# Seven block products for k and v of the second mixer, a halved first piece of expert weights, and two places of the order

## The reference

```python
def heads(t):
    return t.reshape(b, n, h, d).transpose(0, 2, 1, 3)
q = _phi(heads(x @ Wq + bq))          # _phi(t) = elu(t) + 1
k = _phi(heads(x @ Wk + bk))
v = heads(x @ Wv + bv)
kv = jnp.einsum('bhnd,bhne->bhde', k, v)
...
```

```python
importance = jax.lax.stop_gradient(probs).sum(axis=0)
...
balanced = topk_probs / balance
balanced = balanced / balanced.sum(axis=-1, keepdims=True)
```

## Time and profile before

| | us |
|---|---|
| median of 3 runs | 2670.67 |
| lowest, highest | 2668.65, 2671.88 |
| the profiled execution, its own time | 2667.01 |
| its span in the profile | 2665.3 |
| TensorE busy | 2586.9 |
| VectorE busy | 1546.5 |
| ScalarE busy | 780.0 |
| mean granted clock of TensorE | 0.993 of 2.4 GHz |

### The profile page before, as it was taken

How to read it: one execution, slowest core, us unless ns; L and a number is a source line. 1 busy time by engine, 2 the same in 40 slices (tenths; PEclk the granted TensorE clock), 3 DMA queues, 4 the chain that set the end, 5 groups by cost and what they waited for, 6 DMA issues and landing times.

```text
span 2665.3 us, 26854 instructions
## 1 busy us (share of the span) xinstructions
PE 2586.9 (97%) x10727; PEld 1835.0 (69%) x10727; DVE 1546.5 (58%) x2637; ACT 780.0 (29%) x1314; POOL 347.5 (13%) x197
## 2 busy tenths in 40 slices
PE   7999999999999998999999999999999999999999
PEld 4667676658966987777777775555755786556676
DVE  4556461799947996988888997121342561341322
ACT  1043342017723763322222222420002331432000
POOL 0888888000000000000000000000000000000000
PEclk9999999999999998999999999999999999999999
DMA  8232313542020305000120004000350100212201
GB/s 253 29 40 13 49 5 46 146 145 75 20 59 12 104 19 194 1 1 1 71 101 1 24 24 172 11 0 36 79 161 18 36 1 1 69 69 84 86 24 58
DMA packets 137285, 155.70 MB, mean 58 GB/s; under 512 B 96508, under 2 KB 107606, under 8 KB 135634
## 3 DMA queue, kind: packets, MB, share of 16 engines
q1 hardware_dynamic: 66441, 153.56, 18.5%
q0 software_dynamic: 70720, 0.43, 2.7%
...
## 4 chain that ended last, share of the span: by engine, by line
PE 51%; DVE 7%; ACT 2%; DMA 1%; issue 1%; SPq 0%; DVEq 0%; ACTq 0%
PE psum L517 51%; DVE arena L1834 2%; DVE arena L1836 1%; DVE arena L1835 1%; DVE arena L1827 0%; ACT arena L1100 0%; ACT arena L1105 0%; ACT arena L991 0%; DVE arena L1492 0%; DVE arena L1900 0%; PE psum L528 0%; DVE arena L1334 0%; DVE arena L1833 0%; DVE arena L1826 0%; DVE arena L1859 0%
## 5 line engine op out<-in xcount | busy, mean ns | idle before, releaser
L517 PE MATMUL psum<-arena 128*125 128x384 f32 (+10 forms) x9816 | 2478.1, 414 | 39.3 <-DMA arena<-in_ffn_w 7.9
L517 PEld LDWEIGHTS psum<-arena 128*125 128x125 f32 (+3 forms) x9816 | 1733.3, 188 | 758.3 <-issue 135.7
L2161 POOL DMA_INDIRECT count_matrix<-arena x170 | 342.8, 2017 | 118.9 <-DVE arena L1431 59.4
L1834 DVE RECIPROCAL arena<-arena 128x500 f32<-128x500 f32 x60 | 196.7, 3278 | 2.1
L1584 DVE CUSTOM_DVE_ANT_0 arena<-arena 125x1250 bf16<-125x1250 bf16 (+1 forms) x100 | 139.2, 1457 | 12.9 <-ACT arena L1133 12.3
L2171 POOL MEMSET arena<- 125x60 f32 x1 | 0.2, 207 | 980.5 <-PE psum L517 980.5
L1668 DVE TENSOR_TENSOR arena<-arena 125x1250 f32<-125x1250 f32 x80 | 116.3, 1453 | 18.6 <-ACT arena L1082 18.3
L1079 ACT ACTIVATE arena<-arena 125x1250 f32<-125x1250 f32 x80 | 106.9, 1336 | 53.5 <-PE psum L517 53.2
L1671 DVE SCALAR_TENSOR_TENSOR arena<-arena 125x1250 f32<-125x1250 f32 x80 | 116.9, 1461 | 2.8
L991 ACT ACTIVATE arena<-psum 128x250 f32<-128x250 f32 (+1 forms) x102 | 40.8, 491 | 239.6 <-PE psum L528 239.2
L1225 ACT ACTIVATE arena<-psum,arena 128x250 f32<-128x250 f32 x120 | 49.2, 464 | 200.3 <-PE psum L517 200.3
...
## 6 DMA issues: line engine op xcount, KB each, us to landing
...
arena<-in_gat_w SPq DMA_DIRECT2D x3, 2304.0 KB, 9.8
...
```

The lines of the kernel that those rows point to most:

```text
L517: return pe.matmul(o, lhsT, rhs, start=start, stop=stop, skip_group_check=share)
L1834: now(dve.reciprocal(t_, t_))
L2161: pool.indirect_dma_start(counts[k], bass.IndirectOffsetOnAxis(ap=IDX_I[0:T, c:c + 1].bitcast(U32), axis=0), COUNT_I[0:T, c:c + 1], None, ...
```

## The change

Four parts.

1. **Seven block products for k and v.** A pair of tiles and the two halves of the features and of the columns make a 2 x 2 block product; it is formed from seven products of blocks in place of eight (Winograd's form), each three `mm` of 384 columns. All five pairs of k and the last four of v; the first pair of v stays as it was. A pair uses three banks of the V ring: a is filled by products 1 and 6, then 7, then 4, b by 5, then 3, c by 2. VectorE reads a bank between (`mixer_read`), adding what it holds to one or more outputs in memory. VectorE makes sums of weights (3 x 3 x 384 in `TK`, `TV`, and one in place) and of inputs (`XS`, two buffers). k's weight sums stand in VectorE's program behind the second chunk of q; v's behind k's last ELU, the one in place behind v's second tile. `TV` lies over `WF[1]`, so the load of the output weights waits for v's last bank; `TK` lies where v's ones go, so GpSimd's memsets wait for k's last bank.
2. **Half-size first piece.** The first 256 columns of the first expert's weights are loaded as two pieces of 128.
3. **Turns ahead of a norm.** ScalarE copies group 1 of `lng` ahead of the norm of the last two tiles.
4. **Importance mid-chunk.** `imp` stands between the third and the fourth bank of `up1(1)`.

The diff, cut to its core:

```diff
-    V.extend(("k1", t, half) for t in range(NT) for half in range(2))
-    V.extend(("v1", t, half) for t in range(NT) for half in range(2))
+    V.extend(("k1", p, i) for p in range(5) for i in "bca")
+    V.extend(("v1", t, half) for t in range(2) for half in range(2))
+    V.extend(("v1", p, i) for p in range(1, 5) for i in "bca")
...
+        XS = [mem(D_AT + KD * N + i * 1500, 4, 3, T) for i in range(2)]
+        assert D_AT + KD * N + 3000 <= F_AT
+        TK, TV = mem(B_AT, 3, 3, HALF), mem(F_AT + KD * D, 3, 3, HALF)
...
+                            if u == 0 and m == 1:
+                                pe.wait_ge(f1_first[6], 16)
...
+            def mixer_pair(name, p, weight, weight_sums, i, n):
+                low, high = slice(0, 3), slice(3, 6)
+                tile = [slice((2 * p + j) * T, (2 * p + j + 1) * T) for j in range(2)]
+                xs = XS[i % 2]
+                left = [XT[:, low, tile[0]], XT[:, high, tile[0]], xs[:, 3], XT[:, high, tile[1]], xs[:, 0], xs[:, 1], xs[:, 2]]
+                right = [weight[:, low, 0:HALF], weight[:, high, 0:HALF], weight[:, high, HALF:], weight_sums[:, 2],
+                         weight_sums[:, 0], weight_sums[:, 1], weight[:, low, HALF:]]
+                bank_b, bank_c, bank_a = (fill("V", (name, p, j)) for j in "bca")
+                def product(j, b, done, begin=False):
+                    for k in range(3):
+                        last = mm(b[0:T, 0:HALF], left[j - 1][:, k, :], right[j - 1][:, k, :], begin and k == 0, k == 2,
+                                  share=True)
+                    last.then_inc(done, 1)
+                product(1, bank_a, mixer_filled, True)
+                pe.wait_ge(x_sums, i + 1)
+                pe.wait_ge(wk_sums if name == "k1" else wv_sums, 1)
+                product(5, bank_b, mixer_filled, True)
+                pe.wait_ge(mixer_read, 4 * n + 1)
+                product(6, bank_a, mixer_filled)
+                pe.wait_ge(mixer_read, 4 * n + 2)
+                product(3, bank_b, v_filled)
+                pe.wait_ge(mixer_read, 4 * n + 3)
+                product(7, bank_a, mixer_filled)
+                product(2, bank_c, v_filled, True)
+                pe.wait_ge(mixer_read, 4 * n + 4)
+                product(4, bank_a, v_filled)
...
+                mixer_pair("k1", p, WF[1], TK, p, p)
             pe.wait_ge(m1w[2], 16)
-            for t in range(NT):
+            for t in range(2):
                 for half in range(2):
                     natural_product("V", ("v1", t, half), WF[0], HALF, XT, n0=half * HALF, tile=t)
+            for p in range(1, 5):
+                mixer_pair("v1", p, WF[0], TV, 4 + p, 4 + p)
             pe.wait_ge(te_used, 18 + 20)
             pe.wait_ge(kvb_zero, 2)
-            pe.wait_ge(v_drained, V_AT[("v1", NT - 1, 1)] + 1)
+            pe.wait_ge(v_drained, V_AT[("v1", 4, "a")] + 1)
...
-            up1(1, range(2, 4))
+            up1(1, (2,))
 
             pe.wait_ge(rp_made, 1)
             b = fill("V", ("imp",))
             for t in range(NT):
                 last = mm(b[:, 0:E1], ONES[0:T, 0:1].to_broadcast([T, 128]), PR[0:T, t, :], t == 0, t == NT - 1)
             last.then_inc(v_filled, 1)
+            up1(1, (3,))
             for c in range(6):
                 if 1 < c < 5:
...
             turn("lng", XT, groups=(0,))
             deviation(2, 2)
+            turn("lng", XT, groups=(1,))
             normalise(2, 2)
-            turn("lng", XT, groups=(1,))
 
...
+            def weight_sums(w, o):
+                w11, w12, w21, w22 = (w[:, 3 * i:3 * i + 3, j * HALF:(j + 1) * HALF] for i in range(2) for j in range(2))
+                now(dve.tensor_tensor(o[:, 0], w12, w11, ALU.subtract))
+                now(dve.tensor_tensor(o[:, 1], w22, o[:, 0], ALU.subtract))
+                now(dve.tensor_tensor(o[:, 2], w21, o[:, 1], ALU.subtract))
+            def last_weight_sum(w, done):
+                dve.tensor_tensor(w[:, 0:3, HALF:], w[:, 3:6, HALF:], w[:, 0:3, HALF:], ALU.subtract).then_inc(done, 1)
+            x_tok = [0]
+            def x_sum(i, part):
+                p, o = (i if i < 5 else i - 4), XS[i % 2]
+                a11, a12, a21, a22 = (XT[:, 3 * k:3 * k + 3, (2 * p + j) * T:(2 * p + j + 1) * T] for j in range(2) for k in range(2))
+                after(x_tok[0])
+                if part == 0:
+                    x_tok[0] = step(dve.tensor_tensor(o[:, 0], a21, a22, ALU.add))
+                elif part == 1:
+                    x_tok[0] = step(dve.tensor_tensor(o[:, 1], o[:, 0], a11, ALU.subtract))
+                elif part == 2:
+                    x_tok[0] = step(dve.tensor_tensor(o[:, 2], a11, a21, ALU.subtract))
+                else:
+                    dve.tensor_tensor(o[:, 3], a12, o[:, 1], ALU.subtract).then_inc(x_sums, 1)
+            def elu(t, half):
+                cols = slice(half * HALF, (half + 1) * HALF)
+                dve.wait_ge(te_made, n_te[0] + 1)
+                k_ = K1[0:T, t, cols]
+                dve.scalar_tensor_tensor(k_, k_, 0.0, TE[n_te[0] % 2][0:T, 0:HALF], ALU.max, ALU.add).then_inc(te_used, 1)
+                n_te[0] += 1
...
+                def first(b, tt, h, done):
+                    dve.tensor_tensor(o(2 * p + tt, h), shape(b[0:T, 0:HALF]), shape(bias[0:T, h * HALF:(h + 1) * HALF]),
+                                      ALU.add).then_inc(done, 1)
+                def add(b, tt, h, done):
+                    dve.tensor_tensor(o(2 * p + tt, h), shape(b[0:T, 0:HALF]), o(2 * p + tt, h), ALU.add).then_inc(done, 1)
+                dve.wait_ge(mixer_filled, 4 * n + 1)
+                first(bank_a, 0, 0, mixer_read)
+                if sums_of is not None:
+                    x_sum(sums_of, 0)
+                dve.wait_ge(mixer_filled, 4 * n + 2)
+                first(bank_b, 1, 1, mixer_read)
+                if elus and p > 0:
+                    elu(2 * p - 2, 0)
+                dve.wait_ge(mixer_filled, 4 * n + 3)
+                first(bank_a, 0, 1, mixer_read)
+                if sums_of is not None:
+                    x_sum(sums_of, 1)
+                if elus and p > 0:
+                    elu(2 * p - 1, 0)
+                dve.wait_ge(v_filled, V_AT[(name, p, "b")] + 1)
+                dve.wait_ge(mixer_read, 4 * n + 3)
+                add(bank_b, 0, 1, v_drained)
+                if sums_of is not None:
+                    x_sum(sums_of, 2)
+                dve.wait_ge(mixer_filled, 4 * n + 4)
+                add(bank_a, 1, 1, mixer_read)
+                if sums_of is not None:
+                    x_sum(sums_of, 3)
+                if elus:
+                    elu(2 * p, 1)
+                dve.wait_ge(v_filled, V_AT[(name, p, "c")] + 1)
+                add(bank_c, 0, 0, v_drained)
+                if elus:
+                    elu(2 * p + 1, 1)
+                dve.wait_ge(v_filled, V_AT[(name, p, "a")] + 1)
+                first(bank_a, 1, 0, v_drained)
+            n_te = [0]
             for c, (n0, n) in enumerate(CH):
                 for m in range(KD):
-                    dve.wait_ge(te_made, n_te + 1)
-                    dve.tensor_tensor(QT1[:, m, n0:n0 + n], TE[n_te % 2][:, 0:n], TR[n_te % 2][:, 0:n],
+                    dve.wait_ge(te_made, n_te[0] + 1)
...
+                if c == 1:
+                    dve.wait_ge(m1w[1], 16)
+                    dve.wait_ge(a_drained, A_AT[("tr", "ln1", 2, KD - 1)] + 1)
+                    weight_sums(WF[1], TK)
+                    last_weight_sum(WF[1], wk_sums)
+                    for part in range(4):
+                        x_sum(0, part)
...
+            dve.wait_ge(m1w[2], 16)
+            weight_sums(WF[0], TV)
+            for part in range(4):
+                x_sum(5, part)
+            for t in range(2):
                 for half in range(2):
                     dve.wait_ge(v_filled, V_AT[("v1", t, half)] + 1)
...
+            last_weight_sum(WF[0], wv_sums)
+            for p in range(1, 5):
+                mixer_pair("v1", p, 4 + p, v1_half, ROW[3], 5 + p if p < 4 else None, False)
...
-            pool.wait_ge(a_filled, A_AT[("q1", KD - 1, 2)] + 1)
+            pool.wait_ge(v_filled, V_AT[("k1", 4, "a")] + 1)
...
-            for i in range(6):
-                m = slice(256 * i, 256 * (i + 1))
+            for i, n0, n in ((0, 0, 128), (6, 128, 128), (1, 256, 256), (2, 512, 256), (3, 768, 256), (4, 1024, 256), (5, 1280, 256)):
+                m = slice(n0, n0 + n)
                 load(W1[:, :, m], w["ffn0_w1"][bass.DynSlice(chosen[0], 1)].rearrange(
                     "e p (k n) -> (e p) k n", k=KD)[:, :, m], f1_first[i])
-                if i == 0:
+                if i == 6:
                     chosen.append(sp.value_load(IDXI[0:1, 1:2], min_val=0, max_val=3))
                     for s in range(2):
...
-            vf(("k1", NT - 1, 1))
+            vf(("v1", 4, "a"))
             load(WF[1], w["mix1_wo"], m1w[3])
```

52 lines of the change are left out of this document (26 added, 26 removed).

## The result

| | us |
|---|---|
| the changed kernel, median of 4 runs | 2641.01 (2640.06 to 2642.76) |
| the kernel before, 4 runs | 2669.66 (2667.53 to 2671.88) |
| ratio | 0.9893 (95%: 0.9881 to 0.9904) |
| profiled execution, its own time and its span | 2642.76, 2641.0 |

The change takes 28.65 us, the forecast was 28.0 (2641.01 us measured, 2642.7 forecast). The profile's own spans differ by only 24.3 us, and I come to that. First the page of the changed kernel, against the earlier trace rows.

A forecast was written before the change was run, and what follows sets the result against it. TensorE, busy 97% of the span, bounds the kernel by its work plus its holes. The terms 17.4 - 0.1 + 1.1 + 4.8 + 1.6 + 3.2 = 28.0 us take the median from 2670.7 to 2642.7 us, range 2637 to 2650.

The forecast's parts named there:

- products of k and v, with their handshakes: Second mixer's k and v: 27 fewer products at 0.646 us save 17.4 us; handshakes between TensorE and VectorE cost 0.
- first piece: First expert's weights: a half-size first load lands earlier, so TensorE waits 1.1 us less.
- turns: Ahead of the last feed-forward part: copying before the norm frees banks, so the hidden product starts 4.8 us earlier.
- gates: Router's gates at the second chunk: importance made mid-chunk removes TensorE's wait of 1.6 us.
- clock behind the turns: Hidden product after the turns: with the hole gone the granted clock does not fall, saving 0.9 us.
- clock behind the gates, and the down stage: Transposes and down product after the gates: with that wait gone the clock does not fall, saving 2.3 us.
- The margin itself (1.3): Gated bank reads in k and v: VectorE may come 1.3 us late before TensorE has to wait.
- The sums ahead of k: VectorE's weight and input sums before k: the last q chunk's banks still come in time, cost 0 (bounds 0 and 1.4).
- Ahead of v: Before v's first block product: the last weight sum must follow a drain, costing 0.1 us (bounds 0 and 0.5).
- this case (up to 2.9 more): After the expert-weights hole: the clock recovers one stretch earlier, up to 2.9 us more; taken as 0.
- Rival (1): Clock falls as before behind the turns, the gates or both: gain 24.8 to 27.1 us, 2643.6 to 2645.9; chance 0.24.
- rival (2): Short TensorE stops between block products bring the clock down in the mixer: 15 us lost, 2658 us; chance 0.04.

The follow-up runs named there:

- late2: The changed kernel with two idle VectorE sums of 375 columns ahead of each gated read of v's last four pairs; 2640.09 us (1 run).
- late4: The changed kernel with four idle VectorE sums of 375 columns ahead of each gated read of v's last four pairs; 2656.07 us (1 run).
- v_all_pairs: The changed kernel with v's first pair also as seven block products, v's weight sums made during k; 2635.52 us (1 run).
- turns_only: The kernel before with only the turns moved ahead of the norm; 2661.74 us (1 run).
- imp_only: The kernel before with only the importance moved mid-chunk, ahead of the fourth bank; 2669.69 us (1 run).
- both_extended: The changed kernel with v's first pair also as block products and the first piece halved by features; 2638.12 us (4 runs), ratio 0.9881 to before.

## Why the prediction was right

The terms, each by the two profiles:

| term | forecast | measured |
|---|---|---|
| products of k and v, with their handshakes | 17.3 | 17.0 |
| first piece | 1.1 | 1.8 |
| turns | 4.8 | 4.9 |
| gates | 1.6 | 1.7 |
| clock behind the turns | 0.9 | 0.9 |
| clock behind the gates, and the down stage | 2.3 | 2.9 |
| the stretch behind the last product | 0 | 0.3 |
| sum | 28.0 | 29.5 |

The remainders give 29.56. Less the 5.3 us that this execution was later ahead of the edits, that is the 24.3 between the spans; the medians, in which that scatter is smaller, give 28.65. So the agreement of 28.0 with 28.65 is a little closer than the terms themselves were: they were short by 1.5.

**Products.** Right. The forecast argued that a pair of k or v is TensorE's work alone as long as VectorE keeps its margin, and late2 and late4 show it: a little past the margin costs 1.6 us in all, 0.9 us past it (2.3 us of sums) 18.5. The margin itself (1.3) was measured as 1.38. The forecast had also counted the input sum and the ELU part that stand ahead of a read; late2's expectation had not.

**The sums ahead of k** cost 0, as taken. They end 8.35 us behind the start of the add they follow (forecast 8.6), and ScalarE was level at the same distance as before. **Ahead of v** the term was mis-sized: 0.3 us in place of 0.1, inside its bounds. Drain and weight sum take 1.9 us there (1813.42 to 1815.36), as reckoned; what is over stands in the two handovers, TensorE to VectorE and back, for which I had put 0.1 in all. v_all_pairs removes it.

**The first piece** was mis-sized: 1.8 in place of 1.1. At the start the gain was 0.85, between the bounds. The estimate of 0.9 from the fit in the Trainium skill (DMA: Bandwidth & Descriptors, Anatomy of one DMA) agrees with it. But 0.85 mixes two things: at 1 KB packets, half the bytes gave 1.49 us by the means (4.77 and 3.28), near the 1.4 that the forecast had from 289 GB/s, and the cut by columns gave 0.6 of it back. The rule in the Trainium skill of 1 MiB or more a DMA (DMA: Bandwidth & Descriptors, Rules for kernel authors) spoke against the split; for this transfer, which TensorE waits for, the runs speak for it. The other 0.97 us came from the clock, which I had taken as unchanged: in the earlier trace rows the stretch 1028:1030, 4.7 to 6.7 us behind TensorE's start, has 0.72; now 1031:1032, 3.3 to 4.3 behind it, has 0.72 and all after it 1.00. By these rows TensorE ran at 1.2 GHz for 5.8 us before and for 3.8 now, and 2.0 us at half speed cost 1.0. The forecast had named this case (up to 2.9 more) and given it nothing. It appeared in all nine kernels with a split first piece and in none of the four with the whole one.

The fall ahead of it says more. Before, then now (columns as above):

```profile
...
1015.00:1016.00 1.00, 0.39 (x2) 0.30 (x2) 0.47 (x4) 0.50 (x1) 0.00 (x0) 0.74 0.00 0
```

```profile
...
1021.00:1022.00 1.00, 0.00 (x0) 0.00 (x0) 0.86 (x7) 0.00 (x0) 0.00 (x0) 0.66 0.00 0
```

So the clock was low from 1015.5 to 1029.1 before, 13.7 us, and from 1021.3 to 1031.6 now, 10.2 us. Read in stretches of half a microsecond, every trace has one of these two lengths: 13.7 in the four with the whole piece, where TensorE starts again 7.6 to 8.1 us behind the fall, and 10.2 in the nine with a split one, where it starts 5.5 to 7.4 behind it. Among the nine the return stands at the same distance from the fall, whenever TensorE starts, so each microsecond of an earlier start is worth only half at the first drained bank. The clock accounts for all of the difference: in each of the thirteen, from TensorE's start to the drained bank it is 5.4 us plus half of the time at 1.2 GHz behind the start. Why the length is one or the other isn't settled, and the fall comes anywhere from 0.3 to 1.2 us behind the router's small product; so the 0.97 stands in every trace but may be chance in part.

**Turns and gates.** Right in mechanism; turns_only and imp_only give each its own share, and show that each fall hung on its own place. One size was short, the clock behind the gates (2.3, measured 2.9 with the down stage): the forecast had 0.3 us for the turns there, and they take 1.87 us now where they took 2.69 (L947, from 2499.40), of which the longer hole ahead of the down product (1.31 for 0.94) takes 0.4 back. The rest is 0.4 us in the down stage. Rival (1) had 0.24 for a hole that stays: it did stay (1.31 us ahead of the down product), and neither the changed kernel nor imp_only shows a fall there. The Trainium skill's section on psum-queue depth-cycling (TensorE: Matmul & The Clock Gate), on which rival (2) stood, is not borne out here: sixteen stops of 0.60 to 1.06 us in 69 us left the clock at full.

**What stays open.** Thirteen traces reach the router's small product at 1015.03 to 1022.67, and the two of the same changed kernel 3.1 us apart. TensorE's waits for L1599 (2.9 us in seven of the traces, 3.8 to 6.7 in six, the largest in the latest) go with it in part. So does the clock: over 470 to 490 us it was 1.00 before, 0.91 in the changed kernel, where TensorE had waited 2.17 us for L1599 at 477.82, and 0.83 in both_extended, the latest. What makes VectorE late there no run shows.
